# Routing between two layers: rows of eight tiles normalised in the first layer's last pair, transposes two tiles to a bank, logits in four banks, VectorE's order changed

## What is computed

```python
x = x + tanh(g_xattn[0]) * xattn0(layernorm(x), ctx)      # 16 heads
x = x + tanh(g_ffn[0])   * moe(layernorm(x))              # 8 experts, top 2
x = x + tanh(g_xattn[1]) * xattn1(layernorm(x), ctx)      # 8 heads
x = x + tanh(g_ffn[1])   * coupled(layernorm(x))
# moe:
logits = xf @ Wr + br
topk_val, topk_idx = top_k(logits, 2)
scores = softmax(topk_val)
out = sum over the two chosen e of scores * ((silu(a) * g) @ W2[e] + b2[e]),  a, g = split(xf @ W1[e] + b1[e])
```

## Time and profile before

| | us |
|---|---|
| three runs | 968.0, 969.36, 969.6 |
| median | 969.36 |
| the profiled execution | 964.45 |
| its span, first to last instruction | 962.7 |
| TensorE busy in the span | 890.0 (92%) |
| VectorE, ScalarE, GpSimd busy | 560.2, 521.9, 351.5 |

### The profile page before, as it was taken

How to read it: one execution, slowest core, us unless ns; L and a number is a source line. 1 busy time by engine, 2 the same in 40 slices (tenths; PEclk the granted TensorE clock), 3 DMA queues, 4 the chain that set the end, 5 groups by cost and what they waited for, 6 DMA issues and landing times.

```text
span 962.7 us, 19673 instructions
## 1 busy us (share of the span) xinstructions
PE 890.0 (92%) x6485; PEld 804.8 (84%) x6486; DVE 560.2 (58%) x1328; ACT 521.9 (54%) x1473; POOL 351.5 (37%) x494
## 2 busy tenths in 40 slices
PE   5789999999998888999999991799999999999996
PEld 3469999999997766999999991799999999987653
DVE  3475555556656673434434345777777777656456
ACT  7376766667766323443443453565556555652555
POOL 2263444444444113212222135655556544453000
PEclk9899999999999878999999995999999999999998
DMA  8000000060000346676777741200000000000002
GB/s 257 1 1 1 2 1 1 14 195 2 0 1 1 106 145 250 230 267 240 254 258 236 263 127 55 48 22 13 24 11 22 11 13 1 2 1 1 1 1 88
DMA packets 37570, 76.17 MB, mean 79 GB/s; under 512 B 5166, under 2 KB 23842, under 8 KB 37378
## 3 DMA queue, kind: packets, MB, share of 16 engines
q1 hardware_dynamic: 34097, 66.03, 20.7%
q0 software_dynamic: 3408, 9.31, 3.0%
HBM read 66.02 MB, written 9.31 MB: 78 GB/s over the span
## 4 chain that ended last, share of the span: by engine, by line
PE 82%; DVE 7%; POOL 4%; DMA 3%; ACT 2%; issue 2%; DVEq 0%; SPq 0%; POOLq 0%
PE banks L524 15%; PE banks L526 14%; PE banks L525 14%; PE banks L1444 14%; PE banks L559 7%; PE banks L550 6%; PE banks L414 3%; PE banks L1709 2%; PE banks L1714 1%; PE banks L1720 1%; PE banks L1702 1%; POOL W L1120 1%; DMA region_b<-in_L_xattn_Wk 1%; PE banks L531 1%; PE banks L1434 1%
## 5 line engine op out<-in xcount | busy, mean ns | idle before, releaser
L1022 ACT ACTIVATE region_a<-banks,negmax 128x154 f32<-128x154 f32 (+1 forms) x384 | 161.8, 436 | 30.5 <-DVE negmax L834 29.6
L1444 PE MATMUL banks<-region_b,region_a 128*128 128x128 f32 x1248 | 147.5, 277 | 1.2 <-ACT region_b L1479 1.2
L1444 PEld LDWEIGHTS banks<-region_b,region_a 128*128 128x128 f32 x1248 | 144.4, 194 | 1.6 <-issue 0.9
L1145 POOL TENSOR_TENSOR region_a<-region_a,recip 128x512 f32<-128x512 f32 x64 | 66.7, 1042 | 163.5 <-PE banks L559 102.0
L834 DVE TENSOR_REDUCE negmax<-banks 128x4 f32<-128x616 f32 (+1 forms) x128 | 100.6, 786 | 39.0 <-PE banks L550 25.6
L1186 POOL TENSOR_TENSOR region_a<-region_a,recip 128x640 f32<-128x640 f32 x64 | 80.3, 1255 | 103.9 <-DVE recip L838 103.7
L1534 DVE SCALAR_TENSOR_TENSOR region_b<-banks,region_a,region_b 128x128 f32<-128x128 f32 x156 | 44.0, 345 | 109.0 <-PE banks L1444 95.9
L559 PE MATMUL banks<-ident,region_a 128*128 128x128 f32 x640 | 91.2, 273 | 7.4 <-POOL region_a L1147 3.7
L559 PEld LDWEIGHTS banks<-ident,region_a 128*128 128x128 f32 x640 | 76.3, 141 | 20.4 <-POOL region_a L1147 6.1
L524 PE MATMUL banks<-xT_high,Wq_high 128*128 128x256 f32 x256 | 79.9, 312 | 9.0 <-POOL Wq_low L1167 5.0
L1004 ACT CAST pT_high<-banks 128x640 fp32r<-128x640 f32 x64 | 44.4, 694 | 66.2 <-PE banks L559 66.2
(11 more groups left out here) (275 smaller groups left out, 2491.9 us busy)
## 6 DMA issues: line engine op xcount, KB each, us to landing
region_a<-in_L_ffn_W SPq DMA_DIRECT2D x39, 1024.0 KB, 5.0
y_slots<-region_b SPq DMA_DIRECT2D x39, 128.0 KB, 4.1
W<-in_L_ffn_W SPq DMA_DIRECT2D x1, 4096.0 KB, 14.8
xn_rows<-region_b SPq DMA_DIRECT2D x1, 2048.0 KB, 8.6
out<-x SPq DMA_DIRECT2D x8, 256.0 KB, 2.2
x<-in_x SPq DMA_DIRECT2D x1, 1536.0 KB, 12.4
region_b<-in_L_xattn_Wq SPq DMA_DIRECT2D x1, 1024.0 KB, 11.6
region_b<-in_L_xattn_Wo SPq DMA_DIRECT2D x1, 1024.0 KB, 14.2
```

Of the source, the lines that this page charges most:

```text
L1022: e = act.activation(into, source, ACT.Exp, bias=negmax[:, n % 2, u:u + 1], accum_out=sums[:, n % 2, u:u + 1])
L1145: pool.tensor_tensor(normed[:, 0:512].rearrange("p (j n) -> p j n", j=4), pr[:, :, 0:P], rc.broadcast_to([P, 4, P]), ALU.mult)
L1444: mm = pe.matmul(banks[:, 2 * r + part, m * P:(m + 1) * P], W1[r][:, k, cols], xgT[:, r, k, :], start=(k == 0), stop=(k == DK - 1))
```

## The change

Rows of tiles 0 to 7 are normalised by VectorE in steps 2 to 7 of the first layer's last pair, into a part of region_b of their own (xn_early); rows 8 to 15 after it (xn_late). TensorE no longer waits for y_done ahead of b1 and the transposes; it transposes two tiles into one bank (n % 3), ScalarE copies 512 columns at once, and the logits of four tiles have a bank each (3, 4, 5, 6), so that VectorE's reading of one bank is no longer waited for. VectorE treats tiles 0 to 7 in one group, then 8 to 11 and 12 to 15. One V unit stands between the last logits and the rank matmuls, the other behind these. The context's sum is taken at the kernel's start, and POOL shifts the context. The rows go to xn_rows in two DMAs. The five splits of W2 stand behind the weights.

```diff
-        KV1_BANKS = (6, 7) + 2 * (0, 1, 2, 3) + (7, 0) + (4, 5)
+        KV1_BANKS = (7, 6) + 2 * (0, 1, 2, 3) + (7, 0) + (4, 5)
         KV1_FREE = (0, 0) + (0, 0, 0, 0, 3, 4, 5, 6) + (2, 7) + (0, 0)
...
+                    if L is L0 and last and n > 1:
+                        if n == 2:
+                            dve.wait_ge(sem("q2_ps"), GROUPS)
+                            dve.wait_ge(sem("rstd_out"), EARLY)
+                        for row in ((0,), (1,), (2,), (3,), (4, 5), (6, 7))[n - 2]:
+                            normalized_row(dve, row)
...
         def pe_routing(pe):
-            pe.wait_ge(sem("y_done"), NT)
             pe.wait_ge(sem("wr_in"), 48)
             pe.transpose(banks[:, 5, 0:E * 2 * HK], b1_rows, ident[0:E * 2 * HK, 0:E * 2 * HK]).then_inc(sem("b1_ps"), 1)
-            pe_kv1(pe, (0, 1))
-            pe.wait_ge(sem("b1_ready"), 1)
-            for n in range(NT + 3):
-                if n < NT:
-                    pe.wait_ge(sem("xe_ready"), n + 1)
-                    if n >= 4:
-                        pe.wait_ge(sem("xet_sb"), n - 3)
-                    for k in range(DK):
-                        mm = pe.transpose(banks[:, n % 4, k * P:(k + 1) * P], xn_all[:, n, k * P:(k + 1) * P], ident[:])
+            for n in range(PAIRS + 1):
+                if n < PAIRS:
+                    pe.wait_ge(sem("xe_ready"), 2 * n + 2)
+                    if n >= 3:
+                        pe.wait_ge(sem("xet_sb"), n - 2)
+                    for r in range(2):
+                        for k in range(DK):
+                            mm = pe.transpose(banks[:, n % 3, (2 * r + k) * P:(2 * r + k + 1) * P],
+                                              row_of_tile(2 * n + r)[:, k * P:(k + 1) * P], ident[:])
                     mm.then_inc(sem("xet_ps"), 1)
-                if n >= 3:
-                    t = n - 3
-                    pe.wait_ge(sem("xet_sb"), t + 1)
-                    if t in (8, 12):
-                        pe.wait_ge(sem("either_ready"), t // 4 - 1)
-                    for k in range(DK):
-                        mm = pe.matmul(banks[:, 4 + t // 4 % 2, t * E:(t + 1) * E], xeT[:, t % 4, k, :], Wr[:, k, :],
-                                       start=(k == 0), stop=(k == DK - 1), skip_group_check=True)
-                    mm.then_inc(sem("logit_ps"), 1)
-            pe.wait_ge(sem("either_ready"), NT // 4)
+                if n >= 1:
+                    pe.wait_ge(sem("xet_sb"), n)
+                    if n == 5:
+                        pe.wait_ge(sem("b1_ready"), 1)
+                    if n == 7:
+                        pe.wait_ge(sem("y_done"), NT)
+                    for t in range(2 * n - 2, 2 * n):
+                        for k in range(DK):
+                            mm = pe.matmul(logit_bank(t)[:, t * E:(t + 1) * E], xeT[:, t % 4, k, :], Wr[:, k, :],
+                                           start=(k == 0), stop=(k == DK - 1), skip_group_check=True)
+                        mm.then_inc(sem("logit_ps"), 1)
+            pe.wait_ge(sem("y_done"), NT)
+            pe_kv1(pe, (0,))
+            pe.wait_ge(sem("either_ready"), 3)
             pe.wait_ge(sem("before_ready"), 1)
             pe.matmul(banks[:, 4, 0:NT * E], before[:], either.rearrange("p t e -> p (t e)"), start=True, stop=True)
             pe.matmul(banks[:, 5, 0:NT * E], ones[:], either.rearrange("p t e -> p (t e)"), start=True, stop=True)\
                 .then_inc(sem("rank_ps"), 1)
-            pe_kv1(pe, range(KV1_AFTER_RANK, KV1_AFTER_TOKENS))
+            pe_kv1(pe, range(1, KV1_AFTER_TOKENS))
             pe.wait_ge(sem("kv1_raw"), KV1_AFTER_RANK)
             for n in range(TOP * NT):
...
         def pool_routing(pool):
 
             pool.memset(V1[:, :, 2, :], 0.0).then_inc(sem("v_zero"), 1)
+            pool.wait_ge(sem("o2_ps"), GROUPS)
+            pool.wait_ge(sem("ctx_sum"), 2)
+            rest = KEYS - 2 * P
+            for to, first, keys in ((0, 2 * P, rest), (rest, 0, KEYS)):
+                shifted = pool.tensor_tensor(ctx_shifted[:, :, to:to + keys], ctxT[:, :, first:first + keys],
+                                             ctx_third[:].unsqueeze(2).broadcast_to([CK, 2, keys]), ALU.add)
+            shifted.then_inc(sem("ctx_shifted"), 1)
...
+        def row_of_tile(t):
+            return xn_early[:, t, :] if t < EARLY else xn_late[:, t - EARLY, :]
+
+        def normalized_row(dve, t):
+            dve.tensor_scalar(row_of_tile(t), x[:, t, :], mean_var[:, t, 0:1], rstd[:, t:t + 1],
+                              ALU.subtract, ALU.mult).then_inc(sem("xe_ready"), 1)
+
+        def logit_bank(t):
+            return banks[:, (3, 4, 5, 6)[t // 4], :]
+
         def dve_routing(dve):
...
-            dve.wait_ge(sem("rstd_out"), OUT)
-            for t in range(NT):
-                dve.tensor_scalar(xn_all[:, t, :], x[:, t, :], mean_var[:, t, 0:1], rstd[:, t:t + 1],
-                                  ALU.subtract, ALU.mult).then_inc(sem("xe_ready"), 1)
-
-            dve.wait_ge(sem("o2_ps"), GROUPS)
-            dve.tensor_reduce(ctx_sum, ctxT[:, :, :], AX.X, ALU.add).then_inc(sem("ctx_sum"), 1)
-            dve.wait_ge(sem("ctx_sum"), 1)
...
-            for t0 in range(0, NT, 4):
-                at = slice(t0, t0 + 4)
-                dve.wait_ge(sem("logit_ps"), t0 + 4)
-                link(dve.tensor_tensor(logits[:, at], banks[:, 4 + t0 // 4 % 2, t0 * E:(t0 + 4) * E].rearrange("p (t e) -> p t e", t=4),
-                                       br[:, :].unsqueeze(1).broadcast_to([P, 4, E]), ALU.add))
-                for t in range(t0, t0 + 4):
+            for t in range(EARLY, NT):
+                if t >= NT - 4:
+                    dve.wait_ge(sem("rstd_out"), min(t + 1, OUT))
+                normalized_row(dve, t)
+
+            for t0, t1 in ((0, 8), (8, 12), (12, NT)):
+                at, n = slice(t0, t1), t1 - t0
+                for t in range(t0, t1, 4):
+                    dve.wait_ge(sem("logit_ps"), t + 4)
+                    last = dve.tensor_tensor(logits[:, t:t + 4],
+                                             logit_bank(t)[:, t * E:(t + 4) * E].rearrange("p (t e) -> p t e", t=4),
+                                             br[:, :].unsqueeze(1).broadcast_to([P, 4, E]), ALU.add)
+                link(last)
+                for t in range(t0, t1):
                     last = dve.max(top[:, t, :], logits[:, t, :])
                 link(last)
-                for t in range(t0, t0 + 4):
+                for t in range(t0, t1):
                     last = dve.max_index(top_at[:, t, :], top[:, t, :], logits[:, t, :])
                 link(last)
...
-            for piece in range(5):
-                W2_rest(dve, piece, 12 + piece)
...
             dve.tensor_tensor(weight[:, 3, :], weight[:, 1, :], weight[:, 2, :], ALU.mult).then_inc(sem("weight_ready"), 1)
+            for piece in range(5):
+                W2_rest(dve, piece, 12 + piece)
 
         def act_routing(act):
             act.wait_ge(sem("b1_ps"), 1)
             act.copy(b1, banks[:, 5, 0:E * 2 * HK].rearrange("p (e m) -> p e m", e=E)).then_inc(sem("b1_ready"), 1)
-            act_kv1(act, (0, 1))
-            for t in range(NT):
-                act.wait_ge(sem("xet_ps"), t + 1)
-                if t >= 4:
-                    act.wait_ge(sem("logit_ps"), t - 3)
-                act.copy(xeT[:, t % 4], banks[:, t % 4, 0:D].rearrange("p (k n) -> p k n", k=DK)).then_inc(sem("xet_sb"), 1)
-            act_kv1(act, range(KV1_AFTER_RANK, KV1_AFTER_TOKENS))
+            for n in range(PAIRS):
+                act.wait_ge(sem("xet_ps"), n + 1)
+                if n >= 2:
+                    act.wait_ge(sem("logit_ps"), 2 * n - 2)
+                half = slice(2 * (n % 2), 2 * (n % 2) + 2)
+                act.copy(xeT[:, half], banks[:, n % 3, :].rearrange("p (r k n) -> p r k n", r=2, k=DK))\
+                    .then_inc(sem("xet_sb"), 1)
+            act_kv1(act, range(KV1_AFTER_TOKENS))
...
-            pool.wait_ge(sem("xn_stored"), 16)
+            pool.wait_ge(sem("xn_stored"), 32)
...
+            stored_rows = xn_rows.rearrange("(t p) d -> p t d", p=P)
+            sp.wait_ge(sem("xe_ready"), EARLY)
+            sp.dma_start(stored_rows[:, 0:EARLY], xn_early).then_inc(sem("xn_stored"), 16)
             sp.wait_ge(sem("o2_ps"), GROUPS)
             load_keys_or_values(sp, 1, 1)
             sp.wait_ge(sem("xe_ready"), NT)
-            sp.dma_start(xn_rows.rearrange("(t p) d -> p t d", p=P), xn_all).then_inc(sem("xn_stored"), 16)
+            sp.dma_start(stored_rows[:, EARLY:NT], xn_late).then_inc(sem("xn_stored"), 16)
             load_attention(sp, 1)
...
+            dve.tensor_reduce(ctx_sum[:], ctxT[:, :, :], AX.X, ALU.add).then_inc(sem("ctx_sum"), 1)
+            dve.wait_ge(sem("ctx_sum"), 1)
+            dve.tensor_scalar_mul(ctx_third[:], ctx_sum[:], -1.0 / (3 * KEYS)).then_inc(sem("ctx_sum"), 1)
```

(7 more changed lines are left out.)

20 lines of the change are left out of this document (13 added, 7 removed).

## The result

The changed kernel took 959.14 us (median of six executions, 956.65 to 965.31) beside 969.45 for the kernel before (968.0 to 969.95): a ratio of 0.9906, 95% interval 0.9881 to 0.9931. The forecast of 966.3, with its range of 962.0 to 970.0, was wrong in size; its sign held. The executions of either kernel don't lie round one value, and the profiled ones are not typical: the changed kernel's took 965.31, its longest of the six.

What follows compares the result with a forecast made beforehand. TensorE, 82% of the chain, was taken as the bound, with the routing between the attention layers delivering the rank result late; the terms summed to −3.1 us, 966.3 on the median, range 962.0 to 970.0.

Steps and rivals of the forecast that it cites:

- Last pair, +0.7: First layer's last pair: rows 4 and 5, ahead of the last reciprocal, add 0.7 us; bounds 0 to 2.9.
- rival D: Last pair: the longer wait makes TensorE's clock fall there, net +3.6 us, 973.0; chance 0.10.
- the further hold-up: Last pair: rows 6 and 7 could delay POOL by 0.4 us each through the shared port, +1.5 instead of +0.7.
- The stage starts earlier: Stage of transposes and logits: first transpose at about 323.3, 3.4 us earlier.
- The stage's length, 15.3: Transposes and logits: 16.1 less a 0.8 us stall, clock falling 5.3 us in; last logits 4.2 us earlier.
- Rival A: Transposes and logits: clock holds at 2.4 GHz to the last logits, rank 9.6 us earlier, about 960; chance 0.07.
- One V unit ahead of the rank, +1.5 at half clock: Between last logits and rank matmuls: the unit takes 3.6 us, sticking out 1.5 beyond VectorE's tail of 2.1.
- The full clock for the rank matmuls: Rank matmuls: run at about the full clock, not half, gaining 0.4 of their 1.26 us.
- Behind the rank: Rank to last masks: VectorE's 15.2 us set the end against TensorE's 13.8; 3.1 us reach the token matmuls.
- The r units' clock: Last V units, behind the token matmuls: full clock could bring up to 1.8 us more; none counted.
- The five W2 splits: Moved behind the weights: gather starts up to 2.5 us earlier, counted 0; bounds 0 and −0.4, or +1.
- The profiled execution against the median, 4.9 us: Whole kernel: profiled 964.45 against median 969.36, put down to luck with the clock, likely in the last pair.

Runs made afterwards that it cites:

- v_late: Changed kernel with the V unit between the last logits and the rank matmuls moved behind the rank matmuls: 960.84 us, ratio 0.9926 to the kernel before.
- upper group: The slower executions of the unchanged kernel before: 59 of 112, mean 969.6 us, none below 967.9.
- lower group: The faster executions of the unchanged kernel before: 53 of 112, mean 964.4 us, none above 966.7.
- the kernel with late rows: Changed kernel with all sixteen rows normalised behind the last pair: 967.54 us, ratio 0.9999 to the kernel before.
- the filler matmuls: Changed kernel with one extra 128-column identity matmul in each of the eight rounds of transposes and logits: 966.69 us, ratio 0.997 to the kernel before.

## Why the prediction was right in sign and wrong in size

**Last pair, +0.7: right for the work, but the clock took more.** POOL's wait grew by 0.64 us, and goes back to 2.64 without rows 4 and 5; rival D's price, which comes on top, is told of below. POOL's second half took 0.85 us in either order, so the further hold-up of the Trainium skill's page "SBUF — State Buffer" (section "Who interferes with whom"), with which the sum would have been +1.5, did not come, though rows 6 and 7 were themselves slower (1.22 us for two, against 0.73 for rows 4 and 5).

**The stage starts earlier: right.** From the last row of x to the first transpose it is 4.2 us less; with the last pair's 0.6, 3.5 net, against 3.4.

**The stage's length, 15.3: the working was near, the assumption was not.** "It fell 5.3 us into this stage; I keep that distance." The distance varies from execution to execution: 4.6, 10.4 and 4.6 us in three traces of the changed kernel, 5.4, 9.8, 6.5, 7.2 and 6.7 in five of before. At the full clock two tiles take 1.28 us now (333.08 to 334.36 in the second trace), at half 2.45 (333.51 to 335.96 in the first), so each microsecond by which the clock holds longer is worth 0.9. Rival A, which I gave 0.07, comes near in the second trace (a stage of 11.5 us against its 9.9), but there too the V unit ran at half and stuck out. Its time, about 960, is near the measured median by coincidence: no trace of the changed kernel held the clock to the last logits. Rival D came true in the first and third, with 3.45 and 3.52 us over the 13.66 of the profiled execution of before, though only 2.1 to 2.2 over the 15.0 of before's four other traces, in which the clock falls in the last pair as well, for 3.4 us. The Trainium skill, page "TensorE: Matmul & The Clock Gate", section "The HAM clock gate", has the throttled state as the default that activity lifts, by which I had weighed D up and A down. The traces agree only in part: the clock did fall in the half-busy last pair, but TensorE also stayed at half through 16.5 and 18.6 us in which it was busy without a gap.

**One V unit ahead of the rank, +1.5 at half clock: right,** +1.28 in all three traces. The full clock for the rank matmuls did not come (0.50 in the window that ends at 349.80): 0.16 gained, not 0.4. **Behind the rank: right,** 15.22 to 15.24 us to the last mask, with TensorE waiting; v_late shows how near TensorE was to setting the end.

**The r units' clock, "the luck of that execution, and I count none of it": wrong.** They are 1.7 us shorter in all three traces of the changed kernel. But the gain is real only because of the next step; in the kernel before the same 1.7 us go with a loss of 4.2 to 5.4.

**The five W2 splits, "I take 0": this is the step that failed.** It is worth 5.2 us on the medians of the changed kernel and 4.9 on the means, because it issues the gather 2.4 us earlier, 2.9 us ahead of the loads instead of 0.5. I had read the gather's 1.68 us of idle TensorE in an execution in which the loads came 2.2 us behind the gather, and bounded the step by what TensorE had left there. I had asked what the splits wait for, not what goes out beside the gather if TensorE is quicker. The changed kernel with this step undone took 964.9: inside the forecast's own range of 963.8 to 968.0, and 1.4 under its value.

**The profiled execution against the median, 4.9 us, "luck with the clock, likely in the last pair": right for 1.4 us of it.** The rest is the gather's, 5.0 to 5.4 in the last row of the upper group's three traces, less 1.7 of the r units, so the upper group had a loss in it that the profiled execution didn't show and that the change removes. (That execution was also 1.6 to 2.8 us quicker ahead of the last reciprocal, and 1.5 to 1.9 slower behind the stretch.)

**The sum.** Against the upper group (sums of 76.3 to 76.5) the changed kernel's three traces (70.4, 63.7, 71.1; mean 68.4) gain 8.0 us. By rows of the table, means of three traces each: last pair +1.4, first transpose −4.2, stage −1.1, rank +1.3, totals −0.2, second matmul −5.2. Against the lower group (71.7 and 72.1) they gain 3.5. Less the 0.65 of the rows ahead of the stretch that is 7.4 and 2.8. The 2.8 is near the forecast's 3.1, in part by luck: the last pair cost 2.7 us there instead of 0.7, and the r units gave the 1.7 that I hadn't counted. The times are of the same size: their mean over executions went from 967.9 to 960.4 where both were run together, with 23 of the 35 of before in the upper group.

**Open.** What decides how long the clock holds in the stage or whether it falls in the last pair is not known; no trace is of the group at 957 that has eight of the 19 executions; and that rows 4 and 5 cause rival D is likely, not shown.

## What to carry to other kernels

Where the profiled execution is far from the median, the difference may be a bottleneck that the trace doesn't show, as here: find it before a sum is made, by a second trace if one can be had. A move that "frees" a small gather or an idle engine is to be read together with the large loads that the same semaphore lets go: a quicker engine can release them into the one transfer on the path. The early rows were worth several times the work that was moved (7.8 us in the times against some 1.5); by one trace, because TensorE went into the stage without a gap.

## What the runs showed of the hardware

- An indirect gather of one tile took 3.0 us from issue to landing where the loads went out 2.2 us behind it or were held back until it had landed, and 5.8 to 6.2 when two loads of 1 MB were issued 0.5 and 0.95 us behind it (four traces). In the trace of the upper group with the loads held back, TensorE had its rows 3.17 us behind the issue.
- TensorE at half clock stayed there while it was busy without a gap: 18.6 us in the kernel with late rows, 16.5 with the filler matmuls, all in the stage of transposes and 8-column logits; in the same stage of the changed kernel the clock held for 4.6, 10.4 and 4.6 us.
- The same program differs by 5 us between executions (964.4 and 969.6). In its five traces 1.7 us on TensorE, of the clock, decide whether the loads go out 2.2 or 0.5 us behind the gather.
